# The opening of a fused conditioning and mixture-of-experts kernel: other DMA shapes for the first chunk of x and for W2, the biases on another queue, four more idle transposes

## What is computed

```python
# conditioning
q_emb = relu(cond @ W3 + b3)                       # one row per sample
v_sum = sum(x, axis=tokens, keepdims=True)
h = relu(((64 * x + v_sum) * q_emb[:, None, :]) @ W2 + b2)
# mixture of experts on the rows of h, 64 experts, 6 per token, capacity 64
logits = h @ gate_w.T
y = routed_swiglu(h, softmax(logits), w_gate, w_up, w_down)
shared = silu(h @ sw_gate) * (h @ sw_up) @ sw_down
out = x + y + shared
```

## Time and profile before

| | us |
|---|---|
| three runs: median (lowest to highest) | 1213.14 (1212.65 to 1214.21) |
| the profiled execution's own time | 1213.76 |
| span from its first to its last instruction | 1212.0 |
| TensorE busy in that span | 1204.1 |
| first product with W2 begins | 13.61 |
| both halves of the first chunk are through | 27.66 |

### The profile page before, as it was taken

One profiled execution on the slowest core, in us unless ns is written; L12 is line 12 of the kernel. 1 busy time (PEld: TensorE's weight loads), 2 busy tenths in 40 slices (PEclk: granted clock), 3 DMA queues, 4 the chain that ended last, 5 costly groups with the idle time before them and its releaser, 6 DMA issues.

```text
span 1212.0 us, 15869 instructions
## 1 busy us (share of the span) xinstructions
PE 1204.1 (99%) x5687; PEld 889.1 (73%) x5687; DVE 857.4 (71%) x1868; ACT 329.8 (27%) x631; POOL 271.5 (22%) x246
## 2 busy tenths in 40 slices
PE   8999999999999999999999999999999999999998
PEld 7888888888888888888866666666666666666666
DVE  7998989989889888886656555554655664655652
ACT  4554243433423443244111111110111201111111
POOL 0000000000000000000135355353552453553421
PEclk9999999999999999999999999999999999999999
DMA  8947445372643726246767987989989889889863
GB/s 202 233 113 194 97 124 128 83 176 64 165 106 86 183 74 154 59 135 191 245 228 244 326 291 266 347 264 297 342 251 317 302 281 306 291 307 294 280 145 87
DMA packets 158935, 250.91 MB, mean 207 GB/s; under 512 B 22600, under 2 KB 93640, under 8 KB 157704
## 3 DMA queue, kind: packets, MB, share of 16 engines
q1 hardware_dynamic: 142536, 222.22, 57.8%
q0 software_dynamic: 14048, 25.18, 10.3%
q10 hardware_dynamic: 2272, 2.49, 0.7%
HBM read 197.14 MB, written 61.10 MB: 213 GB/s over the span
## 4 chain that ended last, share of the span: by engine, by line
PE 93%; DVE 4%; DMA 1%; issue 1%; ACT 0%; SPq 0%; DVEq 0%; ACTq 0%
PE bank L1504 23%; PE bank L1505 22%; PE bank L1506 22%; PE bank L1708 12%; PE bank L1723 7%; PE bank L1530 2%; PE bank L1626 1%; PE bank L1627 1%; PE bank L1564 1%; PE bank L1562 1%; DMA wd<-in_L_ffn_w_down_dram 1%; DMA brow<-in_L_cond_b_dram 1%; PE bank L1575 1%; DVE x L946 0%; DVE xpart L950 0%
## 5 line engine op out<-in xcount | busy, mean ns | idle before, releaser
L1504 PE MATMUL bank<-hh,gu 128*128 128x512 f32 x704 | 278.0, 395 | 0.0
L1505 PE MATMUL bank<-hl,gu 128*128 128x512 f32 x704 | 274.2, 390 | 0.0
L1506 PE MATMUL bank<-hh,gu 128*128 128x512 f32 x704 | 274.1, 389 | 0.0
L630 POOL DMA_INDIRECT hg<-table,idx_quarter x128 | 126.3, 987 | 645.6 <-DVE idx_hi L1386 596.1
L1504 PEld LDWEIGHTS bank<-hh,gu 128*128 128x128 f32 x704 | 132.1, 188 | 39.1 <-issue 12.8
L1506 PEld LDWEIGHTS bank<-hh,gu 128*128 128x128 f32 x704 | 132.1, 188 | 27.9
L1505 PEld LDWEIGHTS bank<-hl,gu 128*128 128x128 f32 x704 | 132.2, 188 | 26.2
L698 ACT ACTIVATE ah<-prod 128x512 fp32r<-128x512 f32 x96 | 60.6, 632 | 302.0 <-DVE prod L1046 302.0
L1463 DVE STREAM_TRANSPOSE eactT<-eact 32x96 f32<-32x96 f32 (+1 forms) x512 | 133.9, 261 | 7.9
L1504 PE MATMUL bank<-sdh,ah 128*128 128x512 f32 x320 | 125.9, 393 | 0.0
L1505 PE MATMUL bank<-sdl,ah 128*128 128x512 f32 x320 | 124.7, 390 | 0.0
(11 more groups left out here) (132 smaller groups left out, 1670.7 us busy)
## 6 DMA issues: line engine op xcount, KB each, us to landing
wg<-in_L_ffn_w_gate_dram SPq DMA_DIRECT2D x64, 704.0 KB, 9.5
wu<-in_L_ffn_w_up_dram SPq DMA_DIRECT2D x64, 704.0 KB, 11.1
wd<-in_L_ffn_w_down_dram SPq DMA_DIRECT2D x64, 512.0 KB, 5.3
table<-hrow SPq DMA_DIRECT2D x64, 256.0 KB, 4.3
x<-in_x_dram SPq DMA_DIRECT2D x60, 256.0 KB, 6.9
wd<-in_L_ffn_w_down_dram SPq DMA_DIRECT2D x64, 192.0 KB, 6.0
out_dram<-outst SPq DMA_DIRECT2D x35, 256.0 KB, 4.6
outst<-in_x_dram SPq DMA_DIRECT2D x32, 256.0 KB, 3.3
```

The source lines that it names most:

```text
L630: nc.gpsimd.indirect_dma_start(out=hg[p % 3][:, b, :], out_offset=None, in_=quarters, in_offset=bass.IndirectOffsetOnAxis(ap=idx_quarter[: ...
L1504: nc.tensor.matmul(o, st_h, mv_h, start=first_mm, stop=False)
L1505: nc.tensor.matmul(o, st_h, mv_l, start=False, stop=False)
L1506: return nc.tensor.matmul(o, st_l, mv_h, start=False, stop=last_mm)
```

## The change

Four edits, all in the opening:

1. The first chunk of x comes in blocks of 32 tokens instead of quarters of the features. One DMA (64 KB) fills one block on all 128 partitions, eight DMAs make a half; SyncE and ScalarE issue four of each half.
2. W2 comes by input block k, 256 KB each, onto all 128 partitions, each with a semaphore of its own (`w2_in`). SyncE issues k = 0 and 2, ScalarE 1 and 3, and all four stand ahead of x half 1.
3. The two bias DMAs, with their wait for the cleared `brow`, move from SyncE's list to ScalarE's, behind its x blocks.
4. `keep_clock(5)` becomes `keep_clock(9)`.

The bytes are the same. For x and W2 the source pattern is new: of an x block it has 4 feature quarters outermost, then 32 tokens, then 128 values; of a W2 block 4, then 32 rows, then 512 values. The destination pattern is 128 partitions, then one row.

```diff
-        def w2_rows(q, pair):
-            return rows_of(W2, q)[:, PAIRS[pair], :], w2s[q * SQ:(q + 1) * SQ, PAIRS[pair], :]
+        def w2_block(k):
+            return W2.rearrange("(q k j) o -> k q j o", k=KC, j=SQ)[k], w2s[:, k, :]
+
+        def x_block(b):
+            return xf[b * SQ:(b + 1) * SQ, :].rearrange("i (q c) -> q i c", c=P), x32[:, 0, b, :]
...
 # SyncE
             def begin_x(half):
-                for q in range(2):
-                    src, dst = x_quarter(0, q, half)
+                first = half * (NB // 2)
+                for b in range(first, first + NB // 4):
+                    src, dst = x_block(b)
                     sp.dma_start(dst, src).then_inc(x_begun[half], 16)
-            def begin_w2(pair):
-                for q in range(2):
-                    src, dst = w2_rows(q, pair)
-                    sp.dma_start(dst, src).then_inc(piece_loaded[0] if pair else s.w2_begun, 16)
+            def begin_w2(k):
+                src, dst = w2_block(k)
+                sp.dma_start(dst, src).then_inc(w2_in[k], 16)
...
             begin_x(0)
-            sp.wait_ge(s.bias_cleared, 1)
-            for r, b in enumerate((b3, b2)):
-                sp.dma_start(brow[r * KC:(r + 1) * KC, :].rearrange("k (q j) -> k q j", j=SQ),
-                             b.rearrange("(q k j) -> k q j", k=KC, j=SQ)).then_inc(s.bias_loaded, 16)
             begin_w2(0)
+            begin_w2(2)
             begin_x(1)
-            begin_w2(1)
...
 # ScalarE
             begin_x(0)
-            begin_w2(0)
+            act.wait_ge(s.bias_cleared, 1)
+            for r, b in enumerate((b3, b2)):
+                act.dma_start(brow[r * KC:(r + 1) * KC, :].rearrange("k (q j) -> k q j", j=SQ),
+                              b.rearrange("(q k j) -> k q j", k=KC, j=SQ)).then_inc(s.bias_loaded, 16)
+            begin_w2(1)
+            begin_w2(3)
             begin_x(1)
-            begin_w2(1)
             act.wait_ge(s.presets, 1)
             silu_table()
...
             def order_w2(k):
+                act.wait_ge(w2_in[k], 16)
                 copy(w2p[:, k, :].rearrange("p (o a j) -> p o a j", o=KC, j=SQ),
...
-            act.wait_ge(s.w2_begun, 16 * (P // SQ))
             order_w2(0)
             order_w2(1)
-            act.wait_ge(piece_loaded[0], 16 * len(pieces[0][0]))
             order_w2(2)
             order_w2(3)
...
 # VectorE, x_begin
-                dve.wait_ge(x_begun[half], 16 * (P // SQ))
+                dve.wait_ge(x_begun[half], 16 * (NB // 2))
...
 # TensorE
-            keep_clock(5)
+            keep_clock(9)
```

More of the change, by code:

```diff
@@ L218, in adaln_moe_ffn_kernel @@
             w2_ready = sem("w2_ready")
-            w2_begun = sem("w2_begun")
             bias_cleared = sem("bias_cleared")
@@ L276, in adaln_moe_ffn_kernel @@
         piece_loaded = [sem(f"piece_loaded{n}") for n in range(1 + GT // 2 + 1 + 2)]
+        w2_in = [sem(f"w2_in{k}") for k in range(KC)]
         x_begun = [sem(f"x_begun{h}") for h in range(2)]
@@ L315, in x_quarter @@
             return rows[:, :, q * P:(q + 1) * P], x32[q * SQ:(q + 1) * SQ, n % 2, b, :]
-        pieces = [([w2_rows(q, 1) for q in range(P // SQ)],
+        pieces = [([],
                    [(w2h[:, :, oc * P:(oc + 1) * P].rearrange("p k (a j) -> p k a j", j=SQ),
@@ L766, in split_piece @@
             def split_piece(n, parts=None):
-                act.wait_ge(piece_loaded[n], 16 * len(pieces[n][0]))
+                wait(act, piece_loaded[n], 16 * len(pieces[n][0]))
                 for h_part, _, src in pieces[n][1][parts or slice(None)]:
@@ L773, in begin_x, with begin_w2 @@
             def begin_x(half):
-                for q in range(2, P // SQ):
-                    src, dst = x_quarter(0, q, half)
+                first = half * (NB // 2) + NB // 4
+                for b in range(first, first + NB // 4):
+                    src, dst = x_block(b)
                     act.dma_start(dst, src).then_inc(x_begun[half], 16)
[L778 to L781, removed]
+            def begin_w2(k):
+                src, dst = w2_block(k)
+                act.dma_start(dst, src).then_inc(w2_in[k], 16)
             begin_x(0)
-            begin_w2(0)
+            act.wait_ge(s.bias_cleared, 1)
[4 more added lines that the diff above has]
+            begin_w2(3)
             begin_x(1)
-            begin_w2(1)
             act.wait_ge(s.presets, 1)
```

## The result

The changed kernel takes 1227.32 us (median of 4 runs, 1225.90 to 1230.45) against 1212.90 (4 runs, 1212.65 to 1214.21): 1.0119 times the time before, interval 1.0106 to 1.0131, so 14.4 us slower. The forecast was 1227.6. The profiled execution took 1227.59 us with a span of 1225.8, 13.8 more than the one of before.

A forecast was written before the change was run, and what follows sets the result against it. The opening was taken as bound by what the DMA engines move and their order. TensorE's start at 26.0, two halves of 7.03 and 2.25 for the clock gave +14.7, less 0.2: +14.5, 1227.6 us; range 1219 to 1238 (own 1224 to 1232).

The forecast's parts named there:

- The number of engines: Opening DMAs: x and W2 blocks, 4 outermost against 128, run on four DMA engines instead of sixteen.
- The landings: Opening inputs: x half 0 and biases at about 12 us, W2 pairs at 17.7 and 23.4, x half 1 at 30.5.
- ScalarE's hold: ScalarE's opening queue lets some 130 rows stand, so its last issue is done only at 22.9 us.
- The start: First product with W2: TensorE starts at 26.0 us instead of 13.61, behind ScalarE's late issues.
- The clock: TensorE after resting from about 12 to 26 us: lower clock for the first 4.5 us, costing 2.25 us.
- What sets the end: Product of half 1: x could start it at 33.8 us, but it waits for TensorE, free at 35.3.
- rival B: Opening: four engines, deep ScalarE queue, clock stays up; x half 1 sets the end, +13.2 us, 1226.3; chance 0.12.
- The sum: End of the first chunk's product with W2: 42.3 us instead of 27.66, +14.7; forecast +14.5 after taking off 0.2.
- Almost nothing absorbed elsewhere: Rest of the kernel: at most 5.5 us of TensorE idle time could absorb delay; only 0.2 us taken off.
- Rival A: Opening DMAs: blocks run on sixteen engines after all; not slower, -1.1 us (1212.0), at best -3.2; chance 0.15.
- Rival C: Opening DMAs: four engines, slower, 13.1 GB/s for x and 15.8 for W2; +24.3 us, 1237.4; chance 0.12.
- The idle transposes: Four more ahead of the product with W3: nothing beside the late start; without that wait, -0.3 to +0.2 us.

The follow-up runs named there:

- The kernel with ScalarE not held: Changed kernel with all eight blocks of x half 1 issued by SyncE, none by ScalarE; 1227.87 us, 1.0120 times before.

## Why the prediction was right, and where it was not

*The number of engines: right, and shown.* 12 + 10 transfers with four closings, a share of 0.26, four landings for each W2 block, and, with 2 outermost, half of each. By the Trainium skill, "DMA: Bandwidth & Descriptors", section "Why a DMA increments its semaphore by 16 and not by 1", a DMA runs on the largest number of engines up to 16 that divides the outermost size of both patterns. The traces agree, for 4 against 128 and for 2 against 64.

*The landings: right within 2 us.* x half 0 landed at 11.0 (foretold 12.0), the biases at 11.46 (12), W2 by about 16.5 and 21.8 (17.7 and 23.4), x half 1 at 30.49 (30.5). The engines were faster than I took them: 24 GB/s each for W2 against 23.1, and 86 GB/s over four, 21.5 each, for x half 0 against 18.6. The 18.6 came from dividing by the share, and this reads high for rows of 512 B: 0.29 from 5 to 9 us, where four engines of sixteen are 0.25. That x half 1 still came exactly as foretold is luck. I left out that the second chunk, on sixteen engines, mixes with it, which the shares of 0.41 and 0.74 from 18 to 29 us show; at the 21.5 GB/s of half 0 its 131 KB for each engine would have been through 6.1 us after W2 instead of 8.8.

*ScalarE's hold: right in kind, 3.4 us too long.* Its last issue was in at 19.45, not 22.9. Counted in the trace's DMA records, each of the four engines had by then moved about 201 of ScalarE's 336 rows, so the queue let 135 stand, close to the 130 read from the earlier trace rows (counted in the same way, the kernel before had moved 101 of 224 there, and 123 stood). Of the 3.4 us 2.1 are the time of the 206 rows, foretold for 22.3 and reached at 20.2: the engines were faster, and I had rounded the 206 up to the last of W2. 0.7 are the 4.5 rows fewer that had to be moved. 0.6 I had put for the last issue behind the hold, while the issue ended with it.

*The start: 22.30 instead of 26.0*, from that step alone; from the table load on the chain took 2.82 us where I had 3.1.

*The clock: right, 0.4 us too cheap.* Foretold 2.25, measured 2.66 (9.69 against 7.03); 2.33 where only x went by blocks.

*What sets the end: wrong.* The prediction said that half 1 would wait for TensorE and not for x. x could start it at 33.8, TensorE would be free at 35.3. Measured, the first came at 33.73 and TensorE was free at 31.99. The step that failed is the start, mis-sized by 3.7 us; with it the two ends change places, and the end is that of rival B (x half 1 plus one pair chain), although B's conditions, a deep queue and a clock that stays up, both failed. B's sum gives 40.8 for the end of half 1 and the measured one is 40.87, so the time alone would not have told the two apart. The kernel with ScalarE not held shows it directly: a start 4.1 us sooner changed nothing.

*The sum:* the end of the half came at 33.73 + 7.14 = 40.87 instead of 42.3, L1657 +13.2 instead of +14.7. VectorE's path was foretold at +14.2 and showed +14.1 where the second chunk begins (36.51 against 22.38); L1564 is later by as much. It is this path, and not the end of TensorE's half 1, that was handed on: TensorE waited 0.62 us for it ahead of the second chunk. The prediction had reckoned it, and set it aside because TensorE's end came later in its sum. Span and own time grew by 13.8, the medians by 14.4. The forecast of +14.5 is right to 0.7 us because the wrong holder was only 1.5 us later than the right one.

*Almost nothing absorbed elsewhere: right.* The delay of 14.1 at 49 us is still 13.8 at the end.

*Rival A* fell with the closings and the rate. *Rival C*, slower engines, fell too: four engines by themselves run as fast as the best stretch of sixteen. *The idle transposes:* no gain and no loss on their own that can be told. *The biases on ScalarE's queue:* I had given them no gain, since behind four-engine blocks they land at 11.46, later than before. Behind quarters they land at 6.98 and are worth 1 to 2 us, the one part of the change that is shown to gain.

## What to carry to other kernels

Count the closing packets of a queue before changing the shape of a transfer: what stands outermost in the source decided here how many DMA engines carried it, with 128 or 64 outermost on the other side. 4 outermost, in an opening that is bound by DMA, is what made this change 14.4 us slower. What 128 partitions bring to x and W2 on sixteen engines is not shown, since no run sent them so. A transfer confined to few engines also delays the wide ones behind it, since these are complete only when their share on the busy engines is. Before giving a delay to the first instruction that starts late, work out which of the inputs is the last of all, and follow it on every engine that needs it.

The version with all of x and W2 in quarters and only the biases moved beats both kernels, by 0.1% over the one before.

## What the runs showed of the hardware that was not expected

- Two transfers of the same narrow shape do not spread over different engines: halves of a W2 block, issued one after the other and from both queues, moved 51 GB/s at a share of 0.13, which is two engines in all.
- An engine of few moves at least what it moves among sixteen: W2 at 100 GB/s and a share of 0.26 is 24 GB/s for each, against 23 in the best full stretch.
- Idle transposes raise the clock by themselves: with nine of them the 16 records of the product with W3 took 2.02 to 2.82 us (2.47 in the kernel after), with five 3.75 and 3.36. With x in quarters and W2 by blocks the nine took 1.45 us instead of the 2.13 of the kernel after, and TensorE had done nothing but transposes until then.
- With ScalarE not held, the clock was up at the end of the first half and down again after TensorE had stood for 4.97 us (8.83 us for 32 records); in the kernel after, it stayed up over a wait of 1.74 us (7.14). The last wait does not decide it alone: the clock stayed up over 2.20 us with W2 by whole blocks (7.14) and was down after 2.17 us with half blocks (8.83). In the former the profiled execution shows a mean granted clock of 1.000 and the other three 0.997, so not even the same kernel always does the same.
